# Three bf16 parts of the expert values: by GpSimd's subtractions in SBUF, or by TensorE's in PSUM

## The reference, cut to what matters

```python
x = x + tanh(g_xattn) * xattn(layernorm(x), ctx)
n = layernorm(x)
h = silu(n @ W_up.T + b_up) @ W_down.T + b_down          # (tokens, 128)
q = h @ W_q.T;  sim = einsum('bthn,hkpn', q, keys)       # 2 x 8 x 45 a token
sx, sy = top8 of each half; sc, pk = top8 of sx + sy      # 8 heads x 8 experts
z = h @ down_embed[indices].T                            # 64 values a token
z = silu(z * softmax(sc))
x = x + tanh(g_ffn) * z @ up_embed[indices]
```

## Time and profile before

| what | value |
|---|---|
| median of 3 runs | 1550.59 us (1549.45 to 1551.35) |
| the profiled execution | 1553.44 us, of which its span 1551.6 us |
| PE busy in the span | 1319.1 us (85%) |
| PEld busy | 1124.1 us (72%) |
| DVE busy | 1207.7 us (78%) |
| ACT busy | 647.6 us (42%) |
| POOL busy | 405.8 us (26%), 212 instructions |
| mean granted TensorE clock | 0.912 of full speed |

### The profile page before, as it was taken

How to read it: one execution, slowest core, us unless ns; L and a number is a source line. 1 busy time by engine, 2 the same in 40 slices (tenths; PEclk the granted TensorE clock), 3 DMA queues, 4 the chain that set the end, 5 groups by cost and what they waited for, 6 DMA issues and landing times.

```text
span 1551.6 us, 47202 instructions
## 1 busy us (share of the span) xinstructions
PE 1319.1 (85%) x18620; PEld 1124.1 (72%) x18620; DVE 1207.7 (78%) x4170; ACT 647.6 (42%) x1770; POOL 405.8 (26%) x212
## 2 busy tenths in 40 slices
PE   5967889898888989888899988889898888988746
PEld 3756777777777777777777777777777777777645
DVE  1247888888888888878888887888878888888883
ACT  2433444444443434434354443445344343544311
POOL 2123333122333313233331223332122333213220
PEclk8787999999998999999999998999999999999867
DMA  6004443334454333444344345434335443433445
GB/s 170 1 5 114 118 103 107 99 59 108 118 118 105 104 92 67 106 118 118 95 114 98 62 105 118 118 95 114 92 57 117 118 118 96 112 88 75 95 113 117
DMA packets 300290, 153.22 MB, mean 99 GB/s; under 512 B 278111, under 2 KB 291271, under 8 KB 291911
## 3 DMA queue, kind: packets, MB, share of 16 engines
q1 hardware_dynamic: 300103, 150.29, 40.0%
HBM read 78.44 MB, written 4.72 MB: 54 GB/s over the span
## 4 chain that ended last, share of the span: by engine, by line
issue 65%; POOL 17%; PE 10%; DVE 6%; ACT 1%; DMA 0%; SPq 0%; POOLq 0%; DVEq 0%; ACTq 0%
POOL zl L383 7%; POOL k_diag L370 5%; POOL zll L392 4%; DVE xn L825 3%; PE bank L890 3%; PE bank L1024 2%; POOL rstd L389 1%; PE bank L952 1%; PE bank L880 1%; DVE hot_rT L621 1%; PE bank L867 1%; PE bank L949 1%; DVE hot_c L656 1%; PE bank L940 0%; POOL rstdb L386 0%
## 5 line engine op out<-in xcount | busy, mean ns | idle before, releaser
L867 PEld LDWEIGHTS bank<-z,hot_rT 128*128 128x128 bf16 x2048 | 159.8, 99 | 138.9 <-DVE hot_rT L621 105.8
L867 PE MATMUL bank<-z,hot_rT 128*128 128x32 bf16 x2048 | 169.3, 182 | 102.0 <-DVE hot_rT L621 102.0
L386 POOL TENSOR_TENSOR rstdb<-vepsb,minus_half 128x1 f32<-128x1 f32 x32 | 19.5, 611 | 835.8 <-DVE vepsb L809 835.8
L1024 PE MATMUL bank<-ue,coef 128*128 128x256 f32 x1024 | 232.8, 386 | 6.2 <-ACT coef L437 3.4
L1024 PEld LDWEIGHTS bank<-ue,coef 128*128 128x128 f32 x1024 | 194.4, 192 | 43.7 <-ACT coef L437 18.2
L471 ACT ACTIVATE P<-bank,nbias 128x64 f32<-128x64 f32 x512 | 111.4, 333 | 209.4 <-DVE nbias L639 209.4
L437 ACT ACTIVATE coef<-bank 128x512 f32<-128x512 f32 x128 | 137.5, 1074 | 125.6 <-PE bank L880 122.8
L370 POOL TENSOR_TENSOR k_diag<-kT,head_of 128x1024 f32<-128x1024 f32 x64 | 134.3, 2118 | 204.6 <-ACT kT L437 184.6
L880 PE MATMUL bank<-uc,hot_r 128*128 128x32 bf16 x6144 | 169.0, 177 | 19.8 <-DVE uc L627 15.4
L621 DVE TENSOR_SCALAR hot_rT<-hot_rT,p_iota 128x4096 bf16<-128x4096 bf16 x64 | 183.4, 2866 | 0.0
L880 PEld LDWEIGHTS bank<-uc,hot_r 128*128 128x128 bf16 x6144 | 163.2, 96 | 24.2 <-issue 20.2
(11 more groups left out here) (142 smaller groups left out, 2530.1 us busy)
## 6 DMA issues: line engine op xcount, KB each, us to landing
hot_rT<-expert_rows SPq DMA_DIRECT2D x64, 1024.0 KB, 6.3
xt<-in_x SPq DMA_DIRECT2D x32, 128.0 KB, 3.6
out<-x1k SPq DMA_DIRECT2D x32, 128.0 KB, 4.6
ue<-in_L_ffn_up_embed SPq DMA_DIRECT2D x1, 2048.0 KB, 16.4
ct<-in_ctx SPq DMA_DIRECT2D x32, 32.0 KB, 3.2
z<-in_L_ffn_W_up SPq DMA_DIRECT2D x1, 1024.0 KB, 8.3
expert_rows<-r_h SPq DMA_DIRECT2D x64, 8.0 KB, 1.8
hot_r<-hot_rT SPq DMA_TRANSPOSE x64, 8.0
```

Source lines behind the costliest of these rows:

```text
L867: last = mm(bG[k % 2][:, 32 * (q - 16 * k):32 * (q - 16 * k) + 32], hot_rT[:, q, :], part.rearrange("r (h q) c -> r h q c", h=2)[:, :, q, ...
L1024: last = mm(bG0[:, 0:DM], coef[:, c, :, :].rearrange("r h q -> r (h q)"), ue[:, c, :], start=(c == 0), stop=(c == C - 1))
```

## The change

The parts of the expert values are made where the values are, in PSUM. ScalarE copies a bank to SBUF as bf16 (part 0); TensorE multiplies that part with minus the identity and adds it to the same bank, which then holds the rest; ScalarE copies the rest as bf16 (part 1); TensorE subtracts that too; ScalarE copies what is left (part 2). In place of `z_copy(n)` stand `z_part(n, 0)`, `z_part(n, 1)` and `z_part(n, 2)`, and between them on TensorE `less_part(n, 0)` and `less_part(n, 1)`. For that, `dense` writes a token's four values side by side, so that each matmul's output has a stride of four fp32 in the bank; before, each wrote 128 neighbours. `dense(3)` moves from the end of the turn to stand behind `dense(2)`, and both now stand behind `scatter(0)`. GpSimd's two subtractions go, and so do its two multiplications for `k_diag`: ScalarE writes `k_diag` from PSUM in eight copies, one for each head, with the column of `head_of` as the scale, and there is no `kT`. On VectorE the 16 `max_index` into `topi` stand ahead of the small operations on `besti`. Weights are staged at the start in `hot_rT` and `hot_r`, since `z` and `zl` are gone.

```diff
-                    B.wait("z_sb3")
-                    nc.gpsimd.tensor_tensor(zl[:, side, :, :], z[:, side, :, :], top_half(z[:, side, :, :]), ALU.subtract).then_inc(S["zl_ok"], 1)
...
-                    B.wait("zl_ok")
-                    nc.gpsimd.tensor_tensor(zll[:, side, :, :], zl[:, side, :, :], top_half(zl[:, side, :, :]), ALU.subtract).then_inc(S["zll_ok"], 1)
...
+            step(nc.gpsimd.tensor_scalar(minus_h[:, :], ident[:, :], -1.0, None, ALU.mult))
...
-                def z_copy(n):
+                def z_part(n, part):
+                    made, kept = (("z_pe", "zhi"), ("zrest_pe", "zlo"), ("ztail_pe", "ztail"))[part]
...
-                    Fw.wait(f"z_pe{n}")
-                    copy(z[:, 1 - side, :, 4 * n:4 * n + 4], bS[n % 2][:, :].rearrange("r (c t) -> r t c", c=4), f"z_sb{n}")
+                    Fw.wait_nth(made, n)
+                    copy(zparts[:, 1 - side, part, :, 4 * n:4 * n + 4], bS[n % 2][:, :].rearrange("r (t c) -> r t c", c=4), kept)
...
-                    A.free("kdiag1")
-                    copy(kT[:, :, :], bD[:, 256:512].rearrange("p (a t) -> p a t", a=2), "k_sb")
+                    A.free("s_pe1")
+                    for h in range(8):
+                        last = nc.scalar.activation(k_diag[:, :, :, h, :], bD[:, 256:512].rearrange("p (a b k) -> p a b k", a=2, b=2),
+                                                    ACT.Copy, scale=head_of[:, h:h + 1])
+                    last.then_inc(S["kdiag"], 1)
...
                 def dense(n):
                     Fw.wait("hid_sb")
                     if n >= 2:
-                        Fw.wait(f"z_sb{n - 2}")
+                        Fw.wait_nth("ztail", n - 2)
...
-                        last = mm(bS[n % 2][:, 128 * m:128 * m + 128], deT[:, R * c:R * c + R], hT[:, :], start=True, stop=True)
-                    last.then_inc(S[f"z_pe{n}"], 1)
+                        last = mm(bS[n % 2][:, :].rearrange("r (t c) -> r c t", c=4)[:, m, :], deT[:, R * c:R * c + R], hT[:, :], start=(m == 0), stop=False,
+                                  skip_group_check=True)
+                    last.then_inc(S["z_pe"], 1)
+
+                def less_part(n, part):
+
+                    Fw.wait_nth(("zhi", "zlo")[part], n)
+                    mm(bS[n % 2][:, :], minus_h[:, :], zparts[:, 1 - side, part, :, 4 * n:4 * n + 4],
+                       start=False, stop=(part == 1), skip_group_check=True).then_inc(S[("zrest_pe", "ztail_pe")[part]], 1)
```

More of the change, by code:

```diff
@@ L730, in turn @@
                 if B:
+                    B.wait_apart("top_v")
+                    for l in range(2 * RH):
+                        last = nc.vector.max_index(topi[:, l, :], top[:, l, :], sims[:, side, l, :])
+                    last.then_inc(S["top_i"], 1)
                     B.wait("best_i")
@@ L738, in turn @@
                     nc.vector.tensor_copy(ab_h[:, :], ab_i[:, :, :].rearrange("p a s -> p (a s)")).then_inc(S["ab_ok"], 1)
-                    B.wait_apart("top_v")
-                    for l in range(2 * RH):
-                        last = nc.vector.max_index(topi[:, l, :], top[:, l, :], sims[:, side, l, :])
-                    last.then_inc(S["top_i"], 1)
                 if L:
@@ L857, in gather @@
                     if k == 0:
-                        Ct.wait("zll_ok")
+                        Ct.wait_nth("ztail", 3)
                         Ct.free("y_ok")
@@ L863, in gather @@
                         Ct.wait(f"gm{k - 2}")
-                    parts = [zz[:, cs, :, :].bitcast(H)[:, :, 1::2] for zz in (z, zl)] + [zll[:, cs, :, :]]
                     for q in range(16 * k, 16 * k + 16):
-                        for n, part in enumerate(parts):
+                        for n in range(3):
                             last = mm(bG[k % 2][:, 32 * (q - 16 * k):32 * (q - 16 * k) + 32], hot_rT[:, q, :],
-                                      part.rearrange("r (h q) c -> r h q c", h=2)[:, :, q, :], start=(n == 0), stop=(n == 2))
+                                      zparts[:, cs, n, :, :].rearrange("r (h q) c -> r h q c", h=2)[:, :, q, :], start=(n == 0), stop=(n == 2))
                     last.then_inc(S[f"g_pe{k}"], 1)
@@ L898, in scores @@
                     mm(bS[half][:, :], ident_h[:, :], causal[:, :, :].rearrange("p h k -> p (h k)"), start=True, stop=False)
-                    A.wait(f"kdiag{half}")
+                    A.wait("kdiag")
                     for s in range(2):
@@ L991, in turn @@
                 if Fw:
-                    dense(2)
+                    less_part(0, 0)
+                    less_part(1, 0)
                 if A:
@@ L1004, in turn @@
                     last.then_inc(S["av_pe"], 1)
+                if Fw:
+                    less_part(0, 1)
+                    less_part(1, 1)
                 if Ct:
                     scatter(0)
+                if Fw:
+                    dense(2)
+                    dense(3)
+                if Ct:
                     scatter(1)
+                if Fw:
+                    less_part(2, 0)
+                    less_part(3, 0)
+                if Ct:
                     scatter(2)
@@ L1013, in turn @@
                     last.then_inc(S["oT_pe"], 1)
+                if Fw:
+                    less_part(2, 1)
+                    less_part(3, 1)
                 if Ct:
```

83 lines of the change are left out of this document (39 added, 44 removed).

## The result

| kernel | median (range), us | ratio to before, 95% interval | turn, us |
|---|---|---|---|
| before | 1550.97 (1549.45 to 1552.77) | 1 | 45.2 |
| after | 1762.84 (1760.38 to 1764.79) | 1.1365 (1.1345 to 1.1384) | 52.4 |

The last column is the mean of 29 turns, counted as in the earlier trace rows.

The account below looks back on a forecast made before the run. TensorE was taken to carry the turn: 44.5 us falls to 38.8 without the VectorE waits, then added work, waits and low clock make 48.7 against 45.2. Over 29 turns +102, edges +5: 1658 us, range 1598 to 1730.

Parts of the forecast that it names:

- both stalls of VectorE go, and with them 1.79 + 2.73 us of waiting on TensorE: With GpSimd's large work gone, TensorE no longer waits for `xn1` (1.79 us) and the second half of `hot_rT` (2.73).
- What would be late next: Behind the removed `hot_rT` wait: `hot_T(0)` may wait for its DMA, hidden by later work; `hot_T(1)` ends before `gather(1)`.
- wait for `qT`: Ahead of `scores(0)`: ScalarE's eight `k_diag` copies delay `qT`, so TensorE waits 1.0 us a turn.
- (a): Attention times values: ScalarE copies two parts before the second PT, so TensorE waits 1.7 us a turn.
- (b): `less_part(2,0)` behind `scatter(1)`: its part's copy stands behind `coef_copy(1)` on ScalarE, so TensorE waits 2.0 us.
- (c): `less_part(2,1)` waits for `coef_copy(2)` and a part's copy on ScalarE; TensorE waits 1.8 us a turn.
- (d): End of turn: `top_rep` stands behind `coef_copy(3)` and two parts, so TensorE waits 0.6 us for `xn` and `xn1`.
- eight `less_part`: Added TensorE matmuls of 128x512 bf16, 0.3 us each (ends 0.2 and 0.38): +2.4 us a turn.
- low clock at the end: During "out", behind the waits between scatters: a fall costs 1.1 to 1.2 us, one turn in three, +0.4 us a turn.
- Strided matmuls are slow: Rival: `dense` writing every fourth fp32 runs at half speed, +4.2 us a turn, 1780 us; chance 0.07.
- The bf16 copies write slowly: Rival: ScalarE's part copies take 0.95 us from start to start, +4 us a turn, 1775 us; chance 0.05.
- Short copies: The fast rival: ScalarE's bf16 parts take at most 0.1 to 0.2 us, turn 44.8 us, 1539 us; chance 0.05.

Follow-up runs that it names:

- b_straight: The kernel before with its loop written out, so no jump back; 1527.26 us, ratio 0.9857.
- a_straight: The changed kernel (after) with its loop written out, so no jump back; 1690.07 us, ratio 1.0900.
- b_uc: Before, loop kept: GpSimd's two subtractions wait for VectorE's third `uc`, and the 16 `max_index` into `topi` move ahead of the small `besti` operations; 1405.73 us.
- a_pass4: The changed kernel (after) with four turns in a pass of the loop, so 5 jumps in place of 12; 1716.74 us, ratio 1.1083.
- b_late: Before, loop kept, with GpSimd's two subtractions moved behind the second `hot_T`, one right behind the other; 1520.29 us, ratio 0.9801.

## Why the prediction was wrong in size

The miss of 105 us has two parts, and the version without a jump divides them, since the forecast turn had no jump in it: 1762.8 - 1690.1 = 73 us come from the jump, and 1690.1 - 1658 = 32 us from terms of the turn and its edges. That the time went up was forecast with the right terms, so it was not luck.

**The step that failed** is "both stalls of VectorE go, and with them 1.79 + 2.73 us of waiting on TensorE". It holds for a turn without a jump. In 12 turns TensorE's branch, 3.3 to 3.9 us long in before, ended at about the same time as the first stall, so with the stall gone TensorE still stood, 2.9 us on the mean in place of 1.79. The prediction has no term for the jump. Two things in the prediction hid it. It walked through one turn, the one of the earlier trace rows, and took it for all; and it set the result, 48.7 us, against 45.2, the mean of the earlier trace rows, while the turn that it had walked through was 44.5. Those 0.7 us a turn were the jumps of before, 20 of the 73 us; `b_straight` has a mean turn of 44.4. A sign of the jump was in its own rows: the granted clock of 0.54 and the 3.07 us of `up(0)` in the earlier trace rows are from a turn behind a jump, and it put them down to the wait for `xn1`. In the turn of the earlier trace rows, behind a wait for `xn1` without a jump, `up(0)` takes 1.95 us. What would be late next was asked for `hot_T` and not for `xn1`.

**The turn itself** was forecast at 48.7 us; the short turn of after has 49.6 on TensorE (862.91 - 813.29), and the mean of `a_straight` is 49.7. TensorE's timeline through the middle of a short turn has every forecast wait:

```profile
823.72 1.08 PE L896 MATMUL bank<-k_diag,qT 128*64 128x512 f32 x4 [1.25 <-ACT qT L419]
...
833.60 2.30 PE L908 MATMUL bank<-hT,deT 128*128 128x128 f32 x16
...
836.18 0.82 PE L915 MATMUL bank<-zparts,minus_h 128*128 128x512 bf16 x2
838.60 2.20 PE L1005 MATMUL bank<-v_diag,PT 128*64 128x34 f32 x32 [1.60 <-ACT PT L419]
...
847.83 0.88 PE L915 MATMUL bank<-zparts,minus_h 128*128 128x512 bf16 x2 [1.56 <-ACT zparts L419]
...
851.45 0.88 PE L915 MATMUL bank<-zparts,minus_h 128*128 128x512 bf16 x2 [1.27 <-ACT zparts L419]
...
853.37 1.96 PE L1036 MATMUL bank<-WoT,oT 128*128 128x256 f32 x4
855.12 7.95 PE L1041 MATMUL bank<-ue,coef 128*128 128x256 f32 x32
862.91 0.38 PE L1047 MATMUL bank<-ident,xn 128*128 128x128 f32 x2
```

| term, us a turn | forecast | in this turn |
|---|---|---|
| wait for `qT` | 1.0 | 1.25 |
| (a) wait for the second PT | 1.7 | 1.60 |
| (b) wait for the part, bank 4 | 2.0 | 1.56 |
| (c) the same, second time | 1.8 | 1.27 |
| (d) wait at the end | 0.6 | 0.15 + 0.34 |
| eight `less_part` | 2.4 | 3.1 |
| low clock at the end | 0.4 | 1.3 |

The waits came in the forecast places and are 0.9 us shorter in sum (6.2 for 7.1). A pair of `less_part` holds TensorE 0.72 to 0.83 us (851.45 to the next at 852.17, 840.73 to 841.56), 0.39 each where 0.3 was taken: the high end, and so +0.7. The output projection and "out" take 9.5 us (862.91 - 853.37) where they took 8.2 in the turn of the earlier trace rows (753.75 - 745.51, the start of this row):

```profile
745.51 1.13 PE L1019 MATMUL bank<-WoT,oT 128*128 128x256 f32 x4
```

That is +1.3. The prediction put a fall of the clock behind (b) and (c) at one turn in three; it falls in nearly all of `a_straight` and in four of five of `after`. So this term, 0.4 in the forecast, is the one of the turn that was mis-sized most, and it was the prediction's own sign of being wrong. Together -0.9 + 0.7 + 0.9 is +0.7 of the 0.9 us that this turn is over the forecast; 0.2 us is not traced. The 1.0 us of the mean turn makes 29 of the 32 us, and the edges the rest.

Three small slips are in the sums. (c) is 1.7 us by its own parts, 2.0 less 0.3. The upper end of 1730 leaves out the 12 us of its own edges. And the terms of the fast rival come to 44.4 us or less, not 44.8. None of them decides anything here.

**ScalarE.** The eight copies of `k_diag` take 3.02 us, 2.9 forecast, 0.36 from start to start as worked out. The trace has for them:

```profile
818.36 3.02 ACT L488 ACTIVATE k_diag<-bank,head_of 128x256 f32<-128x256 f32 x8 [2.87 <-PE bank L954]
```

The 0.40 us estimated from the Trainium skill, "ScalarE: Activation LUTs", section "What ACT_TABLE_LOAD costs" (eight are 3.2), is a little high here. One copy takes 489 ns on the mean, as that estimate has it (492); what differs is the overlap of two, 0.13 us where 0.09 was taken. The parts take 609 ns each in the mean of 384, and 0.5 from start to start, as said.

**The rivals.** *Strided matmuls are slow* fell: `dense` takes 2.30 us for 16 instructions with a stride of four fp32, the same 2.30 as in the earlier trace rows. The rule of the Trainium skill, "Advanced Engine Details and Errata", section "Memory Cachelines", is not borne out by this shape. *The bf16 copies write slowly* fell with the 609 ns and the 0.5 us from start to start. *Short copies* fell with them too. None of the three had the jump.

## What to carry to other kernels

Before a wait is taken away, look for what else runs out in the same time, above all a jump back of the loop: compare the turns behind a jump with the others, one by one, and read the `issue` rows ahead of the same instruction and the time of the branch itself; then set like turns against like. A stall of VectorE beside GpSimd can be cured by time, not only by taking the work from GpSimd: put the long GpSimd operation beside VectorE's searches and reductions and keep small operations on which other engines wait out of it. And a chain of short steps between two engines can cost more than its waits: here the large matmuls behind them ran at 1.2 GHz in most turns.

## What the runs showed of the hardware

**A jump back has a price on TensorE.** In all six kernels with a loop, TensorE's branch takes 3.3 to 4.1 us when it jumps back and 0.08 us when the loop ends; on the other engines the jump takes 45 to 67 ns. TensorE's next matmul begins about 0.36 us behind it. With no wait to cover it, TensorE's gap is 2.0 us on the mean in `b_uc` and 3.4 in `a_pass4`, and the work behind it often runs at 1.2 GHz for a while: `up(0)` in 11 of 12 turns of after, in 9 of `b_uc`. In all a jump cost 6.1 us in after, 5.3 with five of them and 4.3 in `b_uc`. It cost 1.7 in before, where a wait covered it, and 2.2 in `b_late`, where the clock fell in 2 turns of 12. The Trainium skill gives a branch 51 to 108 ns ("Advanced Engine Details and Errata", section "Control Flow Timing"). That is near what the other engines show, and TensorE's branch where it does not jump; its jump back takes over 30 times as long.

The queue that carries instructions gives a hint of the cause. The pages of the profile count 182 packets on it in after, 162 with five jumps and 151 without a jump; before has 170 and `b_straight` 149. That is about two packets more for each jump. That instructions are brought in again behind each jump would fit; no run tested it.

**Which operations GpSimd holds.** Beside subtractions on 128x2048 a `TENSOR_SCALAR` on 128x8 took 2.97 us in place of 0.16 and one on 128x256 3.68 in place of 0.41, a `SCALAR_TENSOR_TENSOR` with both inputs in SBUF 2.38 in place of 0.68; `FIND_INDEX8` and the reduction of `smax` from PSUM kept their times. A small size doesn't protect. This agrees with the Trainium skill, "SBUF — State Buffer", section "Who interferes with whom", by which VectorE contends with GpSimd in its two-port modes, where whoever comes second is blocked for the whole instruction, and also when it has two inputs in SBUF.
